# An attention and mixture-of-experts kernel: stage 0's values between its keys, loads in another order, one mask table

## The chip, the cores and the metric

The kernel runs on one core of a Trainium2 chip. The metric is device time in microseconds (us) of one execution. The engines are TensorE (PE for matmuls, PEld for weight loads), VectorE (DVE), ScalarE (ACT), GpSimd (POOL) and SyncE (SP, which only issues DMAs here). GpSimd issues DMAs too, on a queue of its own.

## The reference, cut to what matters

```python
x = x + attention(_gn(x), ...)      # x: (2, 48, 48, 384), float32; _gn: 32 groups over h, w and channels
x = x + experts(_gn(x), ...)

qkv = x @ qkv_w.T + qkv_b           # 12 heads of 32
# 16 register tokens give 16 more keys and values for every query
mask = make_neighbourhood_mask(7, 7, 48, 48)     # 7x7 window, clipped at the borders
scores = einsum('bnqe,bnke->bnqk', q, k_cat) / sqrt(32)
attn = softmax(where(mask_cat, scores, -1e30))
o = einsum('bnqk,bnke->bnqe', attn, v_cat)
return o @ out_w.T + out_b

# experts: 4 experts, hidden size 96 each, softmax router, top 2, gelu
```

## The kernel before, in words

The channels lie on the 128 partitions, 3 blocks of 128 (4 heads) per image. Attention runs in **six stages** (`gi` 0 to 5): stages 0 to 2 are the three head blocks of the first image, 3 to 5 those of the second. A product in fp32 quality is made of three fp16 matmuls per step (high times high, high times low, low times high); so after each projection ScalarE writes the high half from PSUM and VectorE the low half.

The image is cut in six column **tiles** (`s`) of 8 columns, 384 tokens each, and in six row **strips** (`a`) of 8 rows. A stage does this:

- *Keys*, strip by strip (`keys`, TensorE; `keys_high`, ScalarE; `keys_low`, VectorE, which also copies the strip's overlapping windows to `KT`), stored to `kscr` by SyncE. In stage 0 a strip waits for the normalised input (`gn_hi`, `gn_lo_v`), which ScalarE and VectorE are writing strip by strip.
- *Queries*, tile by tile, stored to `qscr` by GpSimd. From stage 1 on the output projection of the stage before (`project_out`) stands between them. In stage 0 ScalarE and VectorE split the other weights there too.
- *Values*, tile by tile, copied out by ScalarE (`values_out`) and stored to `vscr` by GpSimd, three DMAs a tile.
- *Scores against keys, first pass* (`scores`, line 1184): six groups per tile into PSUM, VectorE takes a maximum of each (`maximum`, line 561). After six, `split_maxima` splits them, TensorE turns them (`maxima_turned`), ScalarE copies them (`maxima_out`, tile `MT`) and GpSimd sends them into two rows of `QS` (`maxima_in`), where the second pass subtracts them inside the matmul. Tiles 0 to 2 are done ahead; 3 to 5 inside the loop over strips, in three pairs of steps per tile (`score_units`): tile 4's six in tile 2, tile 5's six in tile 3.
- *Second pass* (`key_scores`, line 1210), exponents on ScalarE (`exps`, line 890), and `weighted` (line 1233), which sums values and, with a matrix of ones, the exponents. VectorE then makes reciprocals and normalises (`reciprocals`, `normalise`).

The order on every engine is the order of the code; nothing is scheduled. SyncE's order in a stage: stores of the keys; then for tiles 0 to 3 keys (`keys_in`) and queries (`queries_in`); queries of tiles 4 and 5; values of tiles 0 and 1 (`values_in`, six DMAs each, waiting for the stores `v_out` of the tile and its right neighbour); then keys of tile 4 (into slot 0, once the second pass of tile 0 is through: `st_mm`), values of 2, keys of tile 5, values of 3, 4, 5. `keys_in` first loads a mask table of 8 rows for tiles 0, 1, 4 and 5, because border tiles have another window. In stage 0 the values of tiles 0 and 1 come before the first scores, and the scores of tile 1 (and 2) wait until the maxima of the tile before are copied (`t_ev`), since they share a bank.

In stages 2 and 5 the input's next normalisation runs beside the tiles: `normalised` (line 493, tile `GT_`) and `low_half` (line 503) on VectorE, two of the three low halves on GpSimd (line 343). GpSimd in stage 0 also adds the output bias to the first image (line 394) and issues the six loads of the second image. After stage 5 comes the experts' layer.

## Time and profile before

| | us |
|---|---|
| three runs | 649.11, 655.11, 649.22 (median 649.22) |
| profiled execution | 652.61, its span 650.8 |
| stage 0: start, keys' matmuls, first values, end | 0, 22.7, 51.4, 106.5 |
| stages 1, 2, 3, 4, 5 begin (rounded) | 106, 182, 265, 340, 417 |
| experts' layer begins (rounded) | 505 |

Granted TensorE clock of the profiled execution: 0.992 of full speed. In the rows further down, a bracket at the end gives the time an engine stood idle before the row and what released it; `SPq` is SyncE's DMA queue of instructions; `ps` is PSUM, `KB` the loaded keys, `QS` the loaded queries with mask and maxima rows, `VR` the loaded values, `MX` the maxima.

### The profile page before, as it was taken

What the parts mean: (1) busy time and instruction counts of PE and PEld (TensorE: products, weight loads), DVE (VectorE), ACT (ScalarE), POOL (GpSimd) and SP (SyncE); (2) the same over time, 40 slices, a digit from 0 to 9 for tenths busy, and PEclk for the clock granted to TensorE, in tenths of its full rate; (3) what the DMA queues carried; (4) which work ended last, traced back from release to release, by engine and by line L of the source; (5) the groups of instructions that cost most, each with busy time, mean ns of one, the idle gap of its engine ahead of it and who ended that gap; (6) DMA issues with size and microseconds to landing.
All of it is one profiled execution on the core that took longest, in us unless ns stands there. A gap on an engine that the chain in (4) does not pass through costs nothing.

```text
span 650.8 us, 22416 instructions
## 1 busy us (share of the span) xinstructions
PE 567.0 (87%) x9227; PEld 396.7 (61%) x9227; DVE 455.8 (70%) x1021; ACT 307.4 (47%) x609; POOL 282.7 (43%) x421
## 2 busy tenths in 40 slices
PE   3578879998899978998899987897987889998998
PEld 2346666677655756657675766655765546665554
DVE  6885575777887689676667767886689886863333
ACT  1762555215633288513563244541578337754221
POOL 3116798254222654436993362223744332413131
PEclk9999999999999999999999999999989999999999
DMA  9869774995339952398527966189551002121213
GB/s 305 188 148 287 201 217 119 230 275 156 98 89 220 256 144 71 87 255 227 154 57 177 260 177 165 35 201 256 170 145 48 2 0 74 38 74 37 74 37 109
DMA packets 131597, 95.44 MB, mean 147 GB/s; under 512 B 67324, under 2 KB 125352, under 8 KB 131496
## 3 DMA queue, kind: packets, MB, share of 16 engines
q1 hardware_dynamic: 121992, 75.18, 44.8%
q0 software_dynamic: 9504, 18.84, 9.3%
q8 instruction: 73, 1.20, 0.8%
q14 instruction: 28, 0.23, 0.1%
HBM read 57.62 MB, written 35.54 MB: 143 GB/s over the span
## 4 chain that ended last, share of the span: by engine, by line
PE 53%; DVE 16%; DMA 9%; SPq 7%; ACT 6%; issue 6%; POOL 2%; ACTq 0%; POOLq 0%; DVEq 0%
PE ps L1070 38%; SPq L271 5%; PE ps L1233 5%; PE ps L1184 4%; DVE MX L561 3%; DMA vscr<-VT 3%; DMA KB<-kscr 3%; PE ps L1210 3%; DVE ST L454 2%; ACT XH L831 2%; ACT PT L890 1%; DVE GT_ L493 1%; DVE SUMT L574 1%; DVE KT L531 1%; DMA kscr<-KT 1%
## 5 line engine op out<-in xcount | busy, mean ns | idle before, releaser
L561 DVE TENSOR_REDUCE MX<-ps 128x2 f32<-128x372 f32 x216 | 108.3, 541 | 63.9 <-PE ps L1184 62.9
L1070 PE MATMUL ps<-XH,WQ 128*128 128x384 f16 x810 | 140.6, 327 | 8.7 <-DVE XH L503 7.8
L1070 PEld LDWEIGHTS ps<-XH,WQ 128*128 128x128 f16 x810 | 77.6, 98 | 62.6 <-ACT XH L831 7.5
L890 ACT ACTIVATE PT<-ps 128x448 f32<-128x448 f32 (+1 forms) x162 | 78.7, 511 | 52.0 <-PE ps L1210 51.6
L1184 PE MATMUL ps<-KB,QS 120*32 120x186 f16 x1728 | 57.8, 250 | 27.0 <-DVE MX L561 10.6
L434 POOL TENSOR_TENSOR KT<-QS,KT 128x384 f16<-128x384 f32 x36 | 34.3, 962 | 95.3 <-ACT KT L983 95.3
L1210 PE MATMUL ps<-QS,KB 122*128 122x112 f16 (+1 forms) x864 | 64.3, 213 | 12.1 <-ACT PT L890 7.7
L1070 PE MATMUL ps<-WQ,XH 128*128 128x128 f16 x972 | 62.4, 222 | 5.2 <-issue 4.9
L381 POOL DMA_DIRECT2D QS<-MT x72 | 37.8, 529 | 59.5 <-ACT MT L880 59.1
L1210 PEld LDWEIGHTS ps<-QS,KB 122*128 122x128 f16 x864 | 43.3, 99 | 33.1 <-ACT PT L890 16.6
L1070 PEld LDWEIGHTS ps<-WQ,XH 128*128 128x128 f16 x972 | 56.0, 99 | 11.2 <-issue 8.8
L1233 PE MATMUL ps<-PT,VR 128*32 128x112 f32 (+1 forms) x1296 | 60.1, 258 | 2.5 <-DMA VR<-vscr 2.5
L1233 PE MATMUL ps<-PT,ONE 128*32 128x112 f32 (+1 forms) x1296 | 59.5, 254 | 0.8 <-issue 0.8
L1070 PE MATMUL ps<-OS,WO 128*128 128x384 f16 x324 | 57.6, 326 | 2.5 <-DVE X L545 1.5
L1070 PE MATMUL ps<-KT,WQ 128*128 128x384 f16 x324 | 58.6, 326 | 0.8 <-DVE X L726 0.5
L1184 PEld LDWEIGHTS ps<-KB,QS 120*32 120x32 f16 x1728 | 31.5, 97 | 43.5 <-DVE MX L561 16.8
L386 POOL TENSOR_TENSOR OS<-ON,OS 128x384 f16<-128x384 f32 x36 | 33.2, 922 | 33.2 <-ACT OS L896 32.9
L719 DVE TENSOR_TENSOR QS<-ps,QS 128x384 f32<-128x384 f32 x36 | 19.7, 555 | 39.1 <-POOL KT L434 14.1
L1070 PEld LDWEIGHTS ps<-OS,WO 128*128 128x128 f16 x324 | 31.0, 98 | 25.0 <-issue 3.0
L1070 PEld LDWEIGHTS ps<-KT,WQ 128*128 128x128 f16 x324 | 30.9, 98 | 23.8 <-DVE X L726 3.4
L394 POOL TENSOR_SCALAR X<-X,SM 128x384 f32<-128x384 f32 x36 | 44.4, 1242 | 0.4
L358 POOL DMA_DIRECT2D qscr<-QT x18 | 13.3, 741 | 71.2 <-DVE QT L537 71.1
(168 smaller groups left out, 1003.3 us busy)
## 6 DMA issues: line engine op xcount, KB each, us to landing
KB<-kscr SPq DMA_DIRECT2D x108, 192.0 KB, 7.0
kscr<-KT SPq DMA_DIRECT2D x72, 192.0 KB, 2.5
VR<-vscr SPq DMA_DIRECT2D x216, 56.0 KB
QS<-qscr SPq DMA_DIRECT2D x108, 96.0 KB, 6.6
out<-X SPq DMA_DIRECT2D x11, 576.0 KB, 3.3
X<-in_x SPq DMA_DIRECT2D x6, 576.0 KB, 7.3
qscr<-QT POOLq DMA_DIRECT2D x18, 192.0 KB, 3.3
qscr<-PT POOLq DMA_DIRECT2D x18, 192.0 KB, 5.3
```

What stands on the lines that cost most here:

```text
L271: sp.dma_start(VR[0:8 * KW, s % 2, a, :], vscr[8 * a:8 * a + 8, CT_ * s:CT_ * s + KW, :]).then_inc(vr_in[s % 2][a // 3], 16)
L381: pool.dma_start(QS[SROWS + part:SROWS + part + 1, :, s * SN:(s + 1) * SN], MT[part * HEADS:(part + 1) * HEADS, s % 2, :]).then_inc(m_in[s ...
L386: nc.gpsimd.tensor_tensor(OS[:, 1, s * SN:(s + 1) * SN], ON[:, s % 2, :], OS[:, 0, s * SN:(s + 1) * SN], ALU.subtract).then_inc(s_["os_lo" ...
L394: nc.gpsimd.tensor_scalar(xs(img, c, s * SN, SN), xs(img, c, s * SN, SN), cols["obx"][:, c:c + 1], None, ALU.add).then_inc(s_["ob_add"], 1)
L434: nc.gpsimd.tensor_tensor(HW[:, m % 2, 1, k, :], HF[:, unit % 2, :], HW[:, m % 2, 0, k, :], ALU.subtract).then_inc(s_["hl"], 1)
L561: V.tensor_reduce(out=MX[:, s % 2, t, 2 * pair:2 * pair + 2], in_=ps[:, S_BANK(s, i), 0:2 * RUN].rearrange("p (h n) -> p h n", h=2), op=AL ...
L719: V.tensor_tensor(HF[:, unit % 2, :], ps[:, 2 + k, 0:SN], GE[:, unit % 2, :], ALU.mult).then_inc(s_["hf"], 1)
L890: A(PTS[n % 4][:, 0:w], ps[:, ST_BANK(n), 0:w], ACT.Exp, scale=SCORE).then_inc(s_["exd"], 1)
L1070: last = mm(bank, lhsT(a, k), rhs(b, k), start=(k == 0 and n == 0), stop=(finish and k == steps - 1 and n == 2))
L1184: last = mm(ps[32 * j:32 * j + 32, S_BANK(s, i), hh * RUN:(hh + 1) * RUN], QS[0:SROWS, h, q0:q0 + 32], KB[0:SROWS, h, slot(s), at:at + RUN ...
L1210: last = mm(ps[:, ST_BANK(n), h * w:(h + 1) * w], KB[0:TROWS, h, slot(s), LEAD + CHUNK * a:LEAD + CHUNK * (a + 1)], QS[0:TROWS, h, s * SN ...
L1233: last = mm(ps[DH * h:DH * (h + 1), bank, CT_ * q0:CT_ * q1], lhsT, PTS[n % 4][:, h * w:(h + 1) * w], start=(a == 0), stop=(a == STRIPS - ...
```

## The change

Five things are changed.

1. In stage 0 the values are made in six blocks of another cut: 16 rows of three tiles instead of one tile (`early_values`). Four blocks follow keys strips 1 to 4, one the first query tile, one the last. Banks are dealt anew for stage 0, and ScalarE's and GpSimd's value copies and stores go between those of the queries.
2. In stage 0 the first scores of tiles 0 to 2 then follow without values between; both first sets of maxima are sent after all value stores.
3. SyncE loads tile 3's keys and queries only after tile 0's scores, then values of tiles 0 and 1, then queries of 4 and 5. The mask tables of `keys_in` are gone: one table stays loaded, and the query side names another row at the borders. The loads of the second image are issued in tiles 3 to 5 of stage 0.
4. In tiles 2 and 3 VectorE takes all six maxima before reciprocals and, in stages 2 and 5, before the normalisation.
5. A key bank is free once VectorE's low half is read (`k_ps`), not after the two window copies (`k_lo`).

TensorE in stage 0, from the first keys strip on, before (`XH,WQ` keys and queries, `WQ,XH` values, `KB,QS` scores of the first pass, `ID,MXH` turned maxima):

```order
L1070 MATMUL ps<-XH,WQ 128x384 x108
L1070 MATMUL ps<-WQ,XH 128x128 x54
L1070 MATMUL ps<-BVH,WO 128x1 x27
L1184 MATMUL ps<-KB,QS 32x186 x48
L1070 MATMUL ps<-WQ,XH 128x128 x54
L1196 MATMUL ps<-ID,MXH 8x128 x3
L1184 MATMUL ps<-KB,QS 32x186 x48
```

and now:

```order
L1080 MATMUL ps<-XH,WQ 128x384 x18
L1080 MATMUL ps<-WQ,XH 128x128 x27
L1080 MATMUL ps<-XH,WQ 128x384 x9
...
L1080 MATMUL ps<-XH,WQ 128x384 x18
L1080 MATMUL ps<-WQ,XH 128x128 x27
L1080 MATMUL ps<-XH,WQ 128x384 x45
L1080 MATMUL ps<-WQ,XH 128x128 x27
L1080 MATMUL ps<-BVH,WO 128x1 x27
L1217 MATMUL ps<-KB,QS 32x186 x72
L1229 MATMUL ps<-ID,MXH 8x128 x3
L1217 MATMUL ps<-KB,QS 32x186 x48
```

The values have moved from between the scores to between keys and queries, and the scores of three tiles stand together.

SyncE's queue in a stage, from the first key load on, before:

```order
L251 DMA KB<-in_ktab 8x4x868
L254 DMA KB<-kscr 32x4x768 x3
L260 DMA QS<-qscr 32x4x384 x3
...
L254 DMA KB<-kscr 32x4x768 x3
L260 DMA QS<-qscr 32x4x384 x9
L271 DMA VR<-vscr 112x1x128 x12
L251 DMA KB<-in_ktab 8x4x868
L254 DMA KB<-kscr 32x4x768 x3
L271 DMA VR<-vscr 112x1x128 x6
```

and now:

```order
L250 DMA KB<-kscr 32x4x768 x3
L256 DMA QS<-qscr 32x4x384 x3
...
L250 DMA KB<-kscr 32x4x768 x3
L256 DMA QS<-qscr 32x4x384 x3
L268 DMA VR<-vscr 112x1x128 x12
L256 DMA QS<-qscr 32x4x384 x6
L250 DMA KB<-kscr 32x4x768 x3
L268 DMA VR<-vscr 112x1x128 x6
```

Six query loads have moved from ahead of the twelve value loads to between them and tile 4's keys; the table load before those keys is gone.

VectorE in stage 2, tile 2, before:

```order
L561 TENSOR_REDUCE MX<-ps 128x2 x3
L493 TENSOR_SCALAR GT_<-X,SM 128x384
L574 STREAM_TRANSPOSE SUMT<-ps 128x384
L575 RECIPROCAL RC<-SUMT 128x12
L561 TENSOR_REDUCE MX<-ps 128x2 x3
L568 TENSOR_SCALAR MXH<-MX 128x3x4
```

and now:

```order
L566 TENSOR_REDUCE MX<-ps 128x2 x6
L573 TENSOR_SCALAR MXH<-MX 128x3x4
L574 SCALAR_TENSOR_TENSOR MXH<-MX,MXH 128x3x4
L497 TENSOR_SCALAR GT_<-X,SM 128x384
L579 STREAM_TRANSPOSE SUMT<-ps 128x384
L580 RECIPROCAL RC<-SUMT 128x12
```

The six maxima stand together, and the normalisation and the reciprocal come behind their split.

The diff, cut:

```diff
+VECTOR, VECTOR_SIX = ((0,), (), (1,), (), (), ()), ((), (), (0,), (1,), (), ())
...
         def kb_count(gi, s):
             if s in (2, 3):
                 return 48 * (gi + 1)
-            return 128 * gi + (64 if s < 2 else 128)
-
-        K_BANK = (4, 6, 2, 3, 5, 7)
-        V_BANK = lambda gi, s: 7 if gi and s == TILES - 1 else 2 + s % 2
-        Q_BANK = lambda s: 2 + s % 2
+            return 96 * gi + (48 if s < 2 else 96)
+        K_BANK = lambda gi, a: (4, 6, 2, 3, 5, 7)[a] if gi else (4, 6)[a % 2]
+        V_BANK = lambda gi, s: (2, 3, 2, 3, 2, 7)[s] if gi else (2, 3, 5, 7, 0, 1)[s]
+        Q_BANK = lambda gi, s: 2 + s % 2 if gi else (4, 6)[s % 2]
...
             def keys_in(gi, s):
-                if s in (0, 1, 4, 5):
-                    kind = {0: 0, 1: 1, 4: 1, 5: 2}[s]
-                    sp.dma_start(KB[112:120, :, slot(s), :], ktab[kind, 16:24].unsqueeze(1).broadcast_to([8, HEADS, SLOTW])
-                                 ).then_inc(kb_in[slot(s)], 16)
...
             def values_in(gi, s):
-                for t in {s, min(s + 1, TILES - 1)}:
+                near = {s, min(s + 1, TILES - 1)}
+                for t in near if gi else [2 * b + half for half in {u // 3 for u in near} for b in range(KC)]:
                     sp.wait_ge(v_out[t], 48 * (gi + 1))
...
-                for s in range(4):
+                for s in range(3):
                     keys_in(gi, s)
                     queries_in(gi, s)
+                sp.wait_ge(s_["s_mm"], 36 * gi + 6)
+                keys_in(gi, 3)
+                queries_in(gi, 3)
+                for s in (0, 1):
+                    values_in(gi, s)
                 for s in (4, 5):
                     queries_in(gi, s)
-                for s in (0, 1):
-                    values_in(gi, s)
...
                 for s in range(TILES):
                     queries_out(gi, s)
-                if gi:
-                    register_values(gi)
-                for s in range(TILES):
+                    if gi == 0 and s > 1:
+                        values_out(0, s - 2)
+                register_values(gi)
+                for s in range(TILES) if gi else (4, 5):
                     values_out(gi, s)
-                    if gi == 0 and s == 1:
-                        register_values(gi)
-                    if s in ((3, 4) if gi == 0 else (2, 4)):
-                        maxima_in(gi, s // 2 - 1 if gi else s - 3)
+                    if gi and s in (2, 4):
+                        maxima_in(gi, s // 2 - 1)
+                if gi == 0:
+                    maxima_in(0, 0)
+                    maxima_in(0, 1)
...
-                        if gi == 0 and a == 3:
-                            c, at = s // 2, s % 2 * 3 * SN
-                            pool.dma_start(xs(1, c, at, 3 * SN), x[1, :, c, at:at + 3 * SN]).then_inc(x_in[1][c][s % 2], 16)
+                        if gi == 0 and s > 2 and a in (1, 4):
+                            c, half = s - 3, a // 4
+                            at = half * 3 * SN
+                            pool.dma_start(xs(1, c, at, 3 * SN), x[1, :, c, at:at + 3 * SN]).then_inc(x_in[1][c][half], 16)
...
             def keys_low(gi, a):
-                link(V.scalar_tensor_tensor(out=KU[:, a % 2, 1, :, 3:3 + W], in0=ps[:, K_BANK[a], 0:SN].rearrange("p (r c) -> p r c", c=W),
+                V.scalar_tensor_tensor(out=KU[:, a % 2, 1, :, 3:3 + W], in0=ps[:, K_BANK(gi, a), 0:SN].rearrange("p (r c) -> p r c", c=W),
...
+                                       op0=ALU.add, op1=ALU.subtract).then_inc(s_["k_ps"], 1)
+                dve.wait_ge(s_["k_ps"], 6 * gi + a + 1)
...
-                        if a == 1 and s:
+                        if a == (3 if s in (2, 3) else 1) and s:
                             reciprocals(gi, s - 1)
...
                         if n:
-                            if a in (0, 2):
-                                normalised(n, s, a // 2)
-                            elif a % 2 and a // 2 not in POOL_K[n]:
-                                low_half(n, s, a // 2)
+                            for k in (VECTOR_SIX if s in (2, 3) else VECTOR)[a]:
+                                normalised(n, s, k)
+                            if a == 5:
+                                low_half(n, s, 1)
...
                 for s in range(TILES):
                     queries_high(gi, s)
+                    if gi == 0 and s:
+                        values_out(0, s - 1)
...
             def queries(gi, s):
                 if s < 2:
-                    pe.wait_ge(s_["k_lo"], 6 * gi + 3 + s)
+                    pe.wait_ge(s_["k_ps"], 6 * gi + (3 if gi else 5) + s)
...
                 for j in range(KC):
-                    if 0 < s < TILES - 1:
+                    if s == 0:
+                        pe.wait_ge(s_["k_ps"], 6 * gi + (8, 11, 12)[j])
+                    elif s < TILES - 1:
...
+            def early_values(e):
+                if e == 4:
+                    pe.wait_ge(s_["kr_lo"], 1)
+                if e == 5:
+                    pe.wait_ge(s_["vr_sb"], 1)
+                b, first = e // 2, 3 * (e % 2)
+                for i in range(KC):
+                    at = (first + i) * SN + b * P
+                    last = split_product(ps[:, V_BANK(0, e), P * i:P * (i + 1)], lambda a, k: xh1(a, k, at, P),
+                                         lambda q, k: WQ[:, 0, q, k, 2 * P:3 * P])
+                last.then_inc(s_["v_mm"], 1)
...
                 if i == 0 and s in (1, 2):
-                    pe.wait_ge(s_["t_ev"], 6 * gi + (s if gi == 0 else s - 1))
+                    if 6 * gi + s - 1 > 0:
+                        pe.wait_ge(s_["t_ev"], 6 * gi + s - 1)
...
+                if gi == 0 and s == 0:
+                    if i == 0:
+                        pe.wait_ge(s_["q_lo"], 6)
+                    if 0 < i < 5:
+                        pe.wait_ge(s_["v_sb"], i + 2)
...
+                    if gi == 0 and 0 < a < STRIPS - 1:
+                        early_values(a - 1)
                 for s in range(TILES):
                     queries(gi, s)
...
+                    if gi == 0 and s == 0:
+                        early_values(4)
...
                 if gi == 0:
-                    all_values(0)
-                    all_values(1)
-                    value_bias()
-                    all_scores(0)
-                    all_values(2)
-                    all_values(3)
-                    maxima_turned(0, 0)
...
+                    early_values(5)
                     value_bias()
...
+                for k in range(6):
+                    for i in range(3):
+                        scores(gi, k // 2, 3 * (k % 2) + i)
+                    if k in ((3, 5) if gi else (2, 4)):
+                        maxima_turned(gi, k // 2 - 1)
+                    if gi:
+                        for b in range(KC):
+                            values(gi, k, b)
...
-        out[16 + c, :, :, c] = BIG
+        out[16 + max(c, 3), 0, :, c] = BIG
+        out[16 + c, 1:TILES - 1, :, c] = BIG
+        out[16 + min(c, 4), TILES - 1, :, c] = BIG
```

## Rows read from the trace of the kernel before

**Rows 1.** Page, parts 1, 2 and 6: busy time, DMA share in 40 slices, query loads.
```profile
PE 567.0 (87%) x9227; PEld 396.7 (61%) x9227; DVE 455.8 (70%) x1021; ACT 307.4 (47%) x609; POOL 282.7 (43%) x421
...
DMA  9869774995339952398527966189551002121213
...
QS<-qscr SPq DMA_DIRECT2D x108, 96.0 KB, 6.6
```

**Rows 2.** Instructions in time (start, us, engine, line; waited, releaser): TensorE, stage 0.
```profile
36.10 1.62 PE L1070 MATMUL ps<-XH,WQ 128*128 128x384 f16 x9 [1.71 <-DVE XH L503]
...
69.16 1.68 PE L1070 MATMUL ps<-WQ,XH 128*128 128x128 f16 x27
...
74.29 0.36 PE L1233 MATMUL ps<-PT,VR 128*32 128x88 f32 x8
...
83.03 0.50 PE L1184 MATMUL ps<-KB,QS 120*32 120x186 f16 x16 [1.33 <-DMA KB<-kscr]
```

**Rows 3.** Busy by stretch: PE, PEld, DVE, ACT, POOL; clock, DMA share, GB/s.
```profile
51.40:71.40 20.00, 15.79 (x339) 14.09 (x339) 10.21 (x26) 3.93 (x10) 12.46 (x23) 0.91 1.02 286
...
62.00:63.00 1.00, 0.59 (x17) 0.62 (x21) 0.04 (x1) 0.15 (x1) 0.91 (x2) 0.50 1.11 255
```

**Rows 4.** Waits of TensorE: total us, times, longest.
```profile
PE ps L1184 <- DVE MX L561: 10.6, 12, 1.8
...
PE ps L1184 <- DMA KB<-kscr: 6.7, 6, 1.7
...
PE ps L1070 <- DVE KT L531: 1.0, 2, 0.7
```

**Rows 5.** Instructions in time: VectorE, stage 0.
```profile
55.53 2.81 DVE L561 TENSOR_REDUCE MX<-ps 128x2 f32<-128x372 f32 x6
```

**Rows 6.** Instructions in time: GpSimd, stage 0.
```profile
52.62 0.71 POOL L358 DMA_DIRECT2D qscr<-QT  x1 [0.38 <-DVE QT L537]
...
58.71 1.57 POOL L365 DMA_DIRECT2D vscr<-WR  x3 [0.64 <-ACT WR L874]
...
63.66 1.04 POOL L381 DMA_DIRECT2D QS<-MT  x2
```

**Rows 7.** Instructions in time: SyncE's queue, stage 0.
```profile
63.89 9.49 SPq L271 DMA_DIRECT2D VR<-vscr  x12
...
76.02 2.12 SPq L254 DMA_DIRECT2D KB<-kscr  x3
```

**Rows 8.** Instructions in time: SyncE's queue, stage 1.
```profile
135.43 5.92 SPq L260 DMA_DIRECT2D QS<-qscr  x9
...
145.91 8.43 SPq L271 DMA_DIRECT2D VR<-vscr  x12
...
154.38 0.48 SPq L251 DMA_DIRECT2D KB<-in_ktab  x1
...
154.91 1.44 SPq L254 DMA_DIRECT2D KB<-kscr  x3
```

**Rows 9.** Chain that ended last, stage 1 (start, us, what).
```profile
140.17 5.68 DMA vscr<-VT
```

**Rows 10.** DMA issues from 150 to 170 us: times, KB, us to landing.
```profile
vscr<-VT POOLq DMA_DIRECT2D x3, 64.0 KB, 2.2
```

**Rows 11.** Instructions in time: TensorE, stages 1 and 5.
```profile
163.03 0.34 PE L1184 MATMUL ps<-KB,QS 120*32 120x186 f16 x8 [0.44 <-DVE MX L561]
...
166.96 0.50 PE L1184 MATMUL ps<-KB,QS 120*32 120x186 f16 x16 [1.23 <-DMA KB<-kscr]
...
454.71 0.81 PE L1184 MATMUL ps<-KB,QS 120*32 120x186 f16 x15 [3.43 <-issue]
```

**Rows 12.** Instructions in time: TensorE, stage 2.
```profile
243.37 0.34 PE L1184 MATMUL ps<-KB,QS 120*32 120x186 f16 x8 [1.77 <-DVE MX L561]
```

**Rows 13.** Instructions in time: VectorE, stage 2.
```profile
234.53 0.47 DVE L493 TENSOR_SCALAR GT_<-X,SM 128x384 f32<-128x384 f32 x1
...
240.51 1.47 DVE L493 TENSOR_SCALAR GT_<-X,SM 128x384 f32<-128x384 f32 x1
```

84 lines of the change are left out of this document (34 added, 50 removed).

## The prediction

> **What bounds the kernel now.** I read the page first, then the busy time by stretch, the instructions of each engine in order of time, the waits, and the chain that ended last. TensorE is busy 87% of the span [rows 1], so a microsecond can be gained only where TensorE stands still or where its work moves under something else. The reader should look for two things: how long TensorE stands before a row, and which engine or queue releases it.
>
> In stage 0 the keys are made in six strips. TensorE multiplies 1.62 us and then stands 1.71 us for VectorE's normalised strip [rows 2]. There are five such gaps, four of them of 1.71 us. From the end of the queries (51.4) to the first score against keys (71.4) TensorE holds the values of six tiles and the scores of three. The scores of tiles 1 and 2 each wait for the maxima of the tile before to be turned and copied. But look at the DMA column of that stretch: it is at 1.02 of the engines' time and 286 GB/s [rows 3]. This stretch is full for the DMA engines too, and that is what most of my doubt hangs on.
>
> In the stages after, TensorE's waits are of three kinds: score maxima on VectorE (10.6 us in 12 waits), the loads of key tiles 4 and 5 (6.7 us in 6) [rows 4], and stalls whose releaser the profile does not show, the longest 3.43 us [rows 11]. The last kind comes and goes between executions and I give the change nothing for it. The tail of the program (from 505 us, the second layer) is not touched.
>
> **Part 1: values of stage 0 between the keys.** Six blocks of 27 matmuls, 1.68 us each [rows 2], leave the stretch after 51.4. Four go into the 1.71 us gaps, where they just fit (1.62 + 1.63 to 1.68 against a period of 3.33): free, if nothing slows the strips. The last two still cost their 1.6 us each, one among the queries and one behind them. With weights, queries and value copies on ScalarE and VectorE in one line, the queries should end about 2.8 us later than now, near 54; that is 1.6 for the block and the rest for queries that now wait for a low half behind a weight split. TensorE then needs only the six score groups of each tile, and the pace is VectorE's: 2.81 us of maxima [rows 5] and 0.4 of splitting, 3.2 per tile. Three tiles from 56 end at 66, against 71.4 now. So the naive gain is 5 us, or 8 with the queries unshifted.
>
> I take 3.0, since two queues come last instead. GpSimd issues every store of values in three pieces, 1.57 us per group [rows 6], and now has six of these and six query stores of about 0.7 each behind one another before the first two maxima: 14 to 15 us of issuing from about 47 to 50, so the maxima go out at about 63.5. Before, the first went out at 63.66 [rows 6]: no earlier. Second, the loads of values for tile 0 used to wait for two stores and began at 63.89 [rows 7]; because a block now holds 16 rows of three tiles, they need blocks 0, 2 and 4, the last of which leaves GpSimd near 62 and lands 2.2 us later on quiet engines [rows 10], or 5.7 on full ones [rows 9]. So they begin between 64 and 67.6. The first weighted sum, at 74.29 now [rows 2], can come at about 71.5. Tile 4's keys, which TensorE waited for at 83.03 [rows 2], were issued at 76.02 [rows 7]; the value loads and now two query tiles stand ahead of them, and the six loads of the second image no longer collide with them. They come 1 to 2 us earlier. Ends for this part: 0 (the stores land at 67.6 and everything follows as today) and -8. The value nearest to the rows of the two queues is -3.0.
>
> **Part 2: load order and one mask table, all six stages.** A table load costs the queue 0.53 us before tile 4's keys (154.38 to 154.91) and the same before tile 5's [rows 8]. Against that, the six loads of query tiles 4 and 5 now stand between the values of tile 1 and the keys of tile 4. Nine such loads took 5.92 us, so six are up to 3.9, or 2.9 at the pace of the three key loads that took 1.44 [rows 8]. Net: tile 4's keys 2.4 to 3.4 later, if the value loads begin when they do now. They should not: they began at 145.91, right when the store of tile 1's values landed, 5.68 us after its issue [rows 8, 9], and such a store lands in 2.2 us when the engines are not full [rows 10]. With six query loads of 96 KB [rows 1] out of the way, at 286 KB per us [rows 3], the engines clear 2.0 us sooner, and some 0.5 more for the two tables ahead of tiles 0 and 1. Both effects nearly cancel at tile 4; tile 5's table load and the shorter backlog leave about 0.4 per stage over five stages. I take -2.0. Ends: -5.3, all key waits after stage 0 (6.7 less 1.33) [rows 2, 4], and +17 (3.4 in each of five).
>
> **Part 3: maxima of tiles 4 and 5 back to back.** In tiles 2 and 3 the reciprocals stand between two batches of three maxima. TensorE waits 0.44 for that [rows 11], in four stages, twice each: 3.5 us. In the first tile of each pair the next key load is what ends last (1.23 us at 166.96) [rows 11], so that gain is eaten there. I take half, -1.8; ends 0 and -3.5.
>
> **Part 4: the second image's normalisation in stages 2 and 5.** There the same wait is 1.77 us [rows 12], and there are four like it, two per stage: 10.6 less 3.5 leaves 7.1 us for them. Between the maxima stands not only the reciprocal but a normalisation that took 1.47 us, while the same instruction six microseconds earlier took 0.47 [rows 13]. The order rows show that it moves behind all six maxima. TensorE's waits should go, but tile 5's keys land close behind and VectorE has hardly a pause in these tiles, so I take -4.0; ends 0 (the keys come last) and -7.1. The Trainium skill (SBUF — State Buffer, "SBUF: two separate sides") says VectorE and GpSimd lock a shared port pair against each other, the loser blocking for the whole instruction. The trace agrees in the 1.47 against 0.47 beside a running GpSimd subtraction; by that rule the moved instruction also becomes 1 us shorter, and the sum would take the whole 7.1.
>
> **Part 5: earlier release of key banks.** The low half now frees its bank before the two window copies. TensorE waited for those copies 1.0 us in two places [rows 4]. I take -0.5, ends 0 and -1.0. The added wait on VectorE for its own result replaces one of the same kind: 0.
>
> **Hidden or moved at nothing.** The six loads of the second image go later but are read only in stage 1; the bias additions cover them. The new semaphore waits on TensorE behind value copies come on banks whose copies were finished one query earlier.
>
> Sum: -3.0 - 2.0 - 1.8 - 4.0 - 0.5 = -11.3 us. The profiled execution took 652.6, the median of the runs is 649.2; the profiled one holds a 3.43 us unexplained stall [rows 11], which accounts for the difference. On the median: 649.2 - 11.3 = 637.9, so **638 us**; a profile like the one before would take 641. Taking the doubts of parts 1 and 4 on either side, this case's own range is 633 to 644.
>
> **The rivals.**
>
> *Tile 4's keys come late (slower).* The value stores land no earlier, and the two query tiles ahead push the keys back by 2.8 (between 2.4 and 3.4) in each of five stages: +14, of which stages 2 and 5, where nothing waits for this tile now, absorb about 1 each: +12. The parts that rely on tile 5's keys halve: -0.9 and -2.0; stage 0 and the bank keep -3.5. Total +5.6: 655 to 656 us. It decides from the point where the store lands less than 2.4 us earlier than today. For it: value loads begin with a landing and are then a solid 8 us of issuing. Against it: the store lands just as the DMA's full stretch ends: of the 40 slices of 16.3 us, the one up to 146 has a 9 and the one behind it a 5 [rows 1]. Chance 0.10. The Trainium skill (DMA: Bandwidth & Descriptors, "Queues, rings and completion order") says each DMA engine takes packets in turn from the queues that have work. By that rule a store on GpSimd's queue does not stand behind the SyncE backlog, so taking loads off that backlog would help less, which is this rival. The 5.68 us against 2.2 shows a share, not a bypass.
>
> *Stage 0 opens up.* The maxima pace holds and stores land fast since fewer loads compete: part 1 is -8 and part 2 is -3.5: 649.2 - 8 - 3.5 - 1.8 - 4.0 - 0.5 = 631.4. Chance 0.14.
>
> *Most of it is hidden (about no change).* The DMA stretch at full share stays what ends stage 0, tile 5's keys swallow parts 3 and 4, and TensorE's clock falls in the new sparse stretch, where it has 1.1 us of work in every 3.2. After 1.7 us of standing still it was granted 0.50, the 1.2 GHz level, at 62 [rows 3]; a first tile at that level would add up to 3 us. Then -3 to -4 is left: 646. Chance 0.18.
>
> The forecast keeps 0.58. **Range:** leaving out the slow rival and the far end of the fast one, 630 to 652. About 1% (6.5 us) is what a measurement here tells from no change: faster means under 642.7, slower over 655.7. Faster: 0.50 of the forecast, 0.13 of the fast rival: 0.63. Slower: most of the first rival and a little of the rest: 0.09. Same: 0.28.
>
> **What will show it.** Part 1: key strips still 3.33 us apart with values between, and the first weighted sum at 71 to 72. Part 2: in stage 1 the value loads begin at a time 2 to 2.5 us earlier relative to the end of the queries, and the wait for tile 4's keys stays near 1 us. If it is over 2.5, the slow rival holds. Parts 3 and 4: no wait for maxima over 0.5 us left, and the normalisation at 0.47 us. I am wrong if TensorE stands as long as before in stage 0 or if the waits for maxima turn into waits for keys.

## The result and the profile after: slower

The changed kernel took 662.6 us (median of 4 runs, 661.2 to 666.8) beside 650.4 us for the kernel before on the same chip: a ratio of 1.0171, with a 95% interval of 1.013 to 1.0212. The forecast was 638 us and its range ended at 652, so both were wrong. Nearest to what came is the slow rival (655 to 656 us): tile 4's keys come late. Its size was too small, and its premise, that the value stores land no earlier, held only in part. Timed again later, the same kernel gave 1.0148 (1.0098 to 1.0198). Ratios in this document leave out executions that fell into a slower state (six of eleven for k1 below, one of five for h2), while the times in us are medians of all.

The profiled execution took 662.64 us, with a span of 660.8 us at a mean granted clock of 0.941 (before: 650.8 at 0.992). The first lines of its page, to be laid beside [rows 1]:

```profile
PE 581.1 (88%) x9227; PEld 411.7 (62%) x9227; DVE 447.9 (68%) x1021; ACT 308.2 (47%) x609; POOL 284.4 (43%) x421
...
PEclk8798679999799998899899998999987899999999
DMA  9769347995319853098534965349662001120212
```

TensorE has the same number of instructions and is busy 14.1 us longer, so they ran at a lower clock. In the DMA row the fifth and sixth slices (65 to 98 us), both 7 in [rows 1], are 3 and 4. Part of that is only work that moved: four of the six loads of the second image were issued there before (76.97 to 93.79), and now the first goes out at 96.30. The waits of TensorE say what it stands for. Columns: total us, times, longest.

```profile
PE ps L1217 <- DMA KB<-kscr: 20.0, 6, 4.5
PE ps L1243 <- ACT PT L895: 10.7, 17, 2.0
...
PE ps L1243 <- DMA QS<-MT: 5.6, 3, 2.8
...
PE ps L1217 <- DVE MX L566: 4.5, 10, 1.5
```

Against [rows 4] the waits for score maxima fell from 10.6 to 4.5 us, which is what parts 3 and 4 were after (but b1 below, which lacks both, has 5.5 us of them). The waits for loaded keys rose from 6.7 to 20.0 us. All six stand before tile 4's first scores, one per stage. SyncE's queue and TensorE in stage 1 (start, us; in brackets the wait and its releaser):

```profile
140.98 2.22 SPq L250 DMA_DIRECT2D KB<-kscr  x3
143.24 1.40 SPq L256 DMA_DIRECT2D QS<-qscr  x3
149.58 8.42 SPq L268 DMA_DIRECT2D VR<-vscr  x12
158.04 3.14 SPq L256 DMA_DIRECT2D QS<-qscr  x6
161.23 1.39 SPq L250 DMA_DIRECT2D KB<-kscr  x3
```

```profile
161.80 0.53 PE L1243 MATMUL ps<-QS,KB 122*128 122x88 f16 x8
166.84 0.81 PE L1217 MATMUL ps<-KB,QS 120*32 120x186 f16 x16 [4.52 <-DMA KB<-kscr]
167.44 0.59 PE L1266 MATMUL ps<-PT,VR 128*32 128x112 f32 x8
```

The fourth row of the queue is the six query loads, 3.14 us of issuing right ahead of tile 4's keys. The chain of waits runs through just these: the store of tile 1's values, twelve value loads, six query loads, the keys' landing.

```profile
144.40 5.12 DMA vscr<-VT
149.58 0.71 SPq L268
...
162.18 4.62 DMA KB<-kscr
166.80 0.04 issue
166.84 0.81 PE ps L1217 x11
```

To compare stages of kernels I count from the first matmul of a stage's own keys (in stage 1 at 107.40 before and 111.63 after). The table has the start of the value loads and of tile 4's keys on SyncE's queue so counted, in us. "Again" is a second profile of the changed kernel, a2 the version of the next section that only puts the six query loads back.

| | stage 1 | 2 | 3 | 4 | 5 | mean |
|---|---|---|---|---|---|---|
| value loads, before | 38.51 | 41.13 | 38.85 | 40.31 | 42.04 | 40.17 |
| changed | 37.95 | 39.38 | 36.64 | 38.26 | 39.95 | 38.44 |
| changed, again | 36.43 | 40.26 | 37.46 | 38.00 | 41.24 | 38.68 |
| a2 | 37.76 | 39.19 | 37.03 | 39.05 | 40.32 | 38.67 |
| keys of tile 4, before | 47.51 | 50.13 | 48.25 | 49.29 | 53.12 | 49.66 |
| changed | 49.60 | 51.90 | 48.92 | 50.95 | 51.75 | 50.62 |
| changed, again | 49.11 | 52.08 | 50.28 | 51.16 | 52.57 | 51.04 |
| a2 | 46.22 | 47.65 | 45.78 | 47.52 | 48.78 | 47.19 |

The value loads do begin sooner than before, by 1.7 us in the mean (0.6 to 2.2) and 1.5 in the second profile (0.8 to 2.3), where the forecast had 2.0 to 2.5. But they begin just as soon in a2. Tile 4's keys are issued 1.0 and 1.4 us later than before, and 3.4 and 3.9 later than in a2. (In stage 5 of the kernel before they are late by another cause: they wait 1.9 us for TensorE's work on tile 0, behind the stall of 3.43 us.) TensorE takes the keys up 2.9, 1.3, -0.1, 1.7 and 1.9 us later than before in stages 1 to 5. In stage 3 it used to come to tile 4 only 0.38 us before the keys were there; now it is there 4.12 us before them. What it gains ahead of tile 4 is waited away at that place.

The stretches around that store and behind the wait, in the columns of [rows 3]:

```profile
144.40:149.50 5.10, 5.10 (x124) 4.52 (x125) 3.23 (x8) 1.59 (x4) 4.46 (x10) 1.00 0.68 200
...
166.80:172.80 6.00, 5.96 (x124) 5.08 (x125) 3.42 (x9) 0.98 (x2) 0.00 (x0) 0.50 0.60 149
```

and the stretch in which the same store was under way before, 5.68 us long [rows 9]:

```profile
140.20:145.90 5.70, 4.76 (x109) 4.06 (x107) 3.33 (x8) 1.45 (x3) 4.19 (x8) 1.00 1.10 302
```

Two things are to be seen. First, with the six query loads gone from ahead of it, the DMA share while the store of stage 1 is under way fell from 1.10 to 0.68, and the store took 5.12 us instead of 5.68. That one is the slowest of this profile, though. The same store where it lies on the chain that ended last in other stages (start, us to landing), before in stages 3 and 4:

```profile
298.13 5.80 DMA vscr<-VT
374.36 5.53 DMA vscr<-VT
```

in the changed kernel in stage 4:

```profile
385.27 3.92 DMA vscr<-VT
```

and in its second profile in stages 1, 4 and 5:

```profile
145.37 3.60 DMA vscr<-VT
386.79 3.65 DMA vscr<-VT
467.75 5.64 DMA vscr<-VT
```

So the store mostly lands sooner, by up to 2.2 us, and not always. Second, in the 6 us behind the wait of 4.52 us the granted clock was 0.50, the 1.2 GHz level: the group of eight at 167.44 takes 0.59 us, and the same group at full clock before, at 160.03, took 0.36.

Stage 0, TensorE:

```profile
68.59 0.82 PE L1243 MATMUL ps<-QS,KB 122*128 122x88 f16 x8 [2.50 <-DMA QS<-MT]
...
72.45 0.52 PE L1266 MATMUL ps<-PT,VR 128*32 128x88 f32 x8 [1.00 <-ACT QT L895]
...
84.92 0.81 PE L1217 MATMUL ps<-KB,QS 120*32 120x186 f16 x16 [2.91 <-DMA KB<-kscr]
...
105.81 0.52 PE L1243 MATMUL ps<-QS,KB 122*128 122x88 f16 x8 [2.79 <-DMA QS<-MT]
```

The first weighted sum comes 1.84 us sooner than in [rows 2], but tile 4's keys come 1.89 us later, and near the end of the stage TensorE waits 2.79 us for maxima. GpSimd issues those. Bias additions and loads of the second image stood around the last maxima before too; now two of these loads, of 576 KB each, go out in the 3.7 us right ahead of them, and the chain has 5.19 us from the maxima's issue to their landing:

```profile
96.30 0.64 POOL L430 DMA_DIRECT2D X<-in_x  x1
96.97 2.46 POOL L395 TENSOR_SCALAR X<-X,SM 128x384 f32<-128x384 f32 x2
99.39 0.58 POOL L430 DMA_DIRECT2D X<-in_x  x1
99.97 1.04 POOL L382 DMA_DIRECT2D QS<-MT  x2
```

Stage lengths in us, before and after: stage 0 106.5 and 110.7; 1: 75.3 and 78.9; 2: 83.3 and 85.3; 3: 74.5 and 76.0; 4: 76.9 and 78.8; 5: 88.8 (with the 3.43 us stall of [rows 11]) and 85.7; the rest the same. Stages 0 to 4 are all longer; stage 5, which held the stall before, is shorter.

### The profile page after: what moved, and what is told of

The parts are those of the page before. It is cut to its first block, busy times and chain, and to the rows that moved or that the text cites. A ratio compares the mean times of both kernels' runs of the same rounds, so it can differ in the third digit from the quotient of the medians.

```text
span 660.8 us, 22403 instructions
## 1 busy us (share of the span) xinstructions
PE 581.1 (88%) x9227; PEld 411.7 (62%) x9227; DVE 447.9 (68%) x1021; ACT 308.2 (47%) x609; POOL 284.4 (43%) x421
## 4 chain that ended last, share of the span: by engine, by line
PE 63%; DVE 10%; DMA 9%; ACT 5%; SPq 5%; issue 4%; POOL 3%; ACTq 0%; POOLq 0%; DVEq 0%
PE ps L1080 42%; PE ps L1266 8%; PE ps L1217 5%; PE ps L1243 4%; DMA KB<-kscr 3%; SPq L268 3%; DVE ST L458 2%; ACT PT L895 2%; POOL vscr L366 2%; DMA QS<-MT 1%; DMA vscr<-VT 1%; DVE MX L566 1%; ACT XH L836 1%; DMA X<-in_x 1%; SPq L250 1%
## 5 line engine op out<-in xcount | busy, mean ns | idle before, releaser
L1080 PE MATMUL ps<-XH,WQ 128*128 128x384 f16 x810 | 143.0, 331 | 3.1 <-DVE PT L542 1.3
L895 ACT ACTIVATE PT<-ps 128x448 f32<-128x448 f32 (+1 forms) x162 | 78.6, 510 | 76.4 <-PE ps L1243 76.2
L1217 PE MATMUL ps<-KB,QS 120*32 120x186 f16 x1728 | 62.2, 266 | 28.3 <-DMA KB<-kscr 20.0
L1243 PE MATMUL ps<-QS,KB 122*128 122x112 f16 (+1 forms) x864 | 68.5, 224 | 18.8 <-ACT PT L895 10.7
L1243 PEld LDWEIGHTS ps<-QS,KB 122*128 122x128 f16 x864 | 47.2, 105 | 41.1 <-ACT PT L895 18.9
L1266 PE MATMUL ps<-PT,VR 128*32 128x112 f32 (+1 forms) x1296 | 64.8, 277 | 3.1 <-DMA VR<-vscr 1.6
L1266 PE MATMUL ps<-PT,ONE 128*32 128x112 f32 (+1 forms) x1296 | 63.5, 272 | 0.0
L1217 PEld LDWEIGHTS ps<-KB,QS 120*32 120x32 f16 x1728 | 34.0, 101 | 43.4 <-DMA KB<-kscr 20.9
L1080 PE MATMUL ps<-WQ,XH 128*128 128x128 f16 x972 | 60.5, 220 | 0.0
```

The lines of the kernel that those rows point to most:

```text
L895: A(PTS[n % 4][:, 0:w], ps[:, ST_BANK(n), 0:w], ACT.Exp, scale=SCORE).then_inc(s_["exd"], 1)
L1080: last = mm(bank, lhsT(a, k), rhs(b, k), start=(k == 0 and n == 0), stop=(finish and k == steps - 1 and n == 2))
L1217: last = mm(ps[32 * j:32 * j + 32, S_BANK(s, i), hh * RUN:(hh + 1) * RUN], QS[0:SROWS, h, q0:q0 + 32], KB[0:SROWS, h, slot(s), at:at + RUN ...
L1243: last = mm(ps[:, ST_BANK(n), h * w:(h + 1) * w], KB[0:TROWS, h, slot(s), LEAD + CHUNK * a:LEAD + CHUNK * (a + 1)], QS[0:TROWS, h, s * SN ...
L1266: last = mm(ps[DH * h:DH * (h + 1), bank, CT_ * q0:CT_ * q1], lhsT, PTS[n % 4][:, h * w:(h + 1) * w], start=(a == 0), stop=(a == STRIPS - ...
```

## The experiments

All ratios are to the kernel before, run beside each version on the same chip (647.9 to 658.6 us in these runs). "T" is tile, "Q" the query loads of tiles 4 and 5.

| version | us | ratio | 95% interval |
|---|---|---|---|
| changed kernel | 662.6 | 1.0171 | 1.0130 to 1.0212 |
| the same, again | 662.2 | 1.0148 | 1.0098 to 1.0198 |
| a1 old order of loads | 645.7 | 0.9892 | 0.9858 to 0.9927 |
| a2 only Q back ahead of the values | 640.8 | 0.9820 | 0.9761 to 0.9879 |
| a3 only T3 at once again | 660.6 | 1.0122 | 1.0070 to 1.0174 |
| b1 kernel before + new order of loads | 665.3 | 1.0185 | 1.0142 to 1.0229 |
| c1 changed + filler; again | 659.6; 659.7 | 1.0100; 1.0101 | 1.0066 to 1.0134; 1.0059 to 1.0143 |
| c2 a2 with maxima as before | 644.3 | 0.9873 | 0.9808 to 0.9938 |
| c3 a2 without early values | 643.4 | 0.9853 | 0.9786 to 0.9921 |
| d1 a2 + stores reordered | 639.1 | 0.9802 | 0.9734 to 0.9871 |
| g1 d1 + filler | 643.4 | 0.9866 | 0.9820 to 0.9913 |
| h1 kernel before + one table | 648.3 | 0.9916 | 0.9881 to 0.9950 |
| h2 h1 + T3 deferred | 641.6 | 0.9836 | 0.9773 to 0.9899 |
| h3 h1 + maxima and bank release | 645.7 | 0.9868 | 0.9816 to 0.9921 |
| k1 d1 + T5's queries behind T4's keys | 650.5 | 0.9861 | 0.9806 to 0.9916 |

### Which part of the new order costs the time: a1, a2, a3, b1

**Theory:** the six query loads between the values and tile 4's keys. **Rivals:** the new arrangement of stage 0, and the deferral of tile 3's loads. In a2 the edit is:

```diff
                 keys_in(gi, 3)
                 queries_in(gi, 3)
-                for s in (0, 1):
-                    values_in(gi, s)
                 for s in (4, 5):
                     queries_in(gi, s)
+                for s in (0, 1):
+                    values_in(gi, s)
```

a1 also loads tile 3 at once, as before; a3 does only that. b1 puts the new order (with T3 deferred and Q behind the values) into the kernel before and changes nothing else.

a1: 

> The changed kernel with SyncE's load order put back (tile 3 and the queries of 4 and 5 right behind tile 2, values after them); all else of the change stays. Theory T (the six query loads between the values and tile 4's keys make those keys late, and the clock falls in the wait): tile 4's keys wait falls from 20.0 us in six waits to under 7, and the time is 643 to 648. Rival R (stage 0's new arrangement and its queues are what costs): stays over 656. Rival C (deferring tile 3 is the cost, the queries do not matter): also 643 to 648; the next two kernels tell it from T.

a2: 

> The changed kernel with only the queries of tiles 4 and 5 moved back ahead of the values; tile 3 stays deferred until tile 0's scores. T: SyncE issues them in its pause before the stores of values land, tile 4's keys come about 3 us earlier per stage, time 645 to 650. Rival C: tile 3's load still meets the stores, so values begin late, time 657 to 663.

a3: 

> The changed kernel with only tile 3 loaded at once; the queries of 4 and 5 stay behind the values. T: the store of tile 1's values lands earlier by 1 to 2 us (less traffic than before), but the six loads keep their 3.2 us ahead of tile 4's keys: 652 to 659. Rival C: 643 to 648.

b1: 

> The kernel before with only the load order of the change (tables still loaded). T: slower than before by 10 us or more, 658 to 668, with long waits for tile 4's keys. Rival R: within 2 us of before.

The pattern leaves no doubt: every version with Q behind the values is at 1.01 or over, every one with Q ahead is under 0.992, whatever the rest. Alone in the old kernel (b1) the new order gives 1.0185, as much as the whole change. Two expectations were missed in size: a2 came out 4 us below the lowest time named for it, a3 some 2 us above the highest. SyncE's queue in a2, stage 1, and TensorE's wait there:

```profile
137.04 5.26 SPq L256 DMA_DIRECT2D QS<-qscr  x9
144.16 8.41 SPq L268 DMA_DIRECT2D VR<-vscr  x12
152.62 2.46 SPq L250 DMA_DIRECT2D KB<-kscr  x3
```

```profile
158.12 0.50 PE L1217 MATMUL ps<-KB,QS 120*32 120x186 f16 x16 [0.89 <-DMA KB<-kscr]
```

Counted from the stage's first keys (106.40) the value loads begin at 37.76, in the changed kernel at 37.95, and in the mean of five stages at 38.67 against 38.44 and 38.68: with the six loads ahead of them they are no later. The keys are issued at 46.22 and not at 49.60. Where tile 3 is loaded at once, the moved queries do buy something in front: the value loads begin at 39.61 in a1 and at 38.48 in a3 (means), but the keys go out at 48.29 and at 50.96. So beside the deferral of tile 3 moving the queries bought nothing at the front and cost 3.4 to 3.9 us at the back. By the ratios that is 21 to 23 us from a2 to the changed kernel (0.9820 to 1.0148 and 1.0171), and 15 us from a1 to a3; the forecast's far end for part 2 was +17. In the profiles each of stages 0 to 4 is 2.6 to 5.2 us longer than in a2 (105.5, 74.9, 80.6, 72.7 and 76.2 us there). The rival of stage 0's arrangement falls with b1, that of the deferral with a3 and a2: with Q ahead, deferring tile 3 does not cost, as a1, without it, is 4.7 us slower than a2. (With Q behind, a3 is 1.7 to 3.2 us faster than the changed kernel, within the intervals.)

b1 has the tables still and none of the other parts, and yet it is as slow as the changed kernel, though with Q ahead the maxima (3.1 and 3.5 us) and the table (5.5 us) alone are worth some 9 us (below). One reason shows in its waits for maxima, which are short without any reordering (10.6 us in the kernel before):

```profile
PE ps L1187 <- DVE MX L564: 5.5, 8, 1.8
```

With TensorE at a lower clock behind each wait for keys, VectorE keeps up, and reordered maxima have less to gain. That is a reading of the two profiles; no run was made for it.

### Does the clock matter: c1, g1, and both again

**Theory clock:** what TensorE loses at 0.50 behind each wait adds to the loss. Rival: behind the wait other engines set the pace anyway. The edit keeps TensorE multiplying until the keys are there; the filler's result is overwritten.

```diff
                 if i == 0 and s == 4:
+                    pe.wait_ge(s_["mx"], 36 * gi + 23)
+                    for _ in range(20):
+                        mm(ps[:, S_BANK(4, 0), 0:SN], WO[:, 0, 0, 0:P], WO[:, 0, 0, :], start=True, stop=True)
```

c1: 

> The changed kernel with 20 extra matmuls (384 columns each, results not used, some 3.2 us) on TensorE just ahead of its wait for tile 4's keys in each stage. They add work only to time in which it stands. Clock theory (part of the loss is the clock that falls to the 1.2 GHz level in these waits of 2 to 4.5 us, then a slow tile of some 2 us more): granted clock of tile 2 stays near 1.00 and the time falls by 5 to 12 us, to 650 to 657. Rival (the waits alone make the loss; the keys come when they come): the same time within 2 us, 660 to 665, or slower.

The changed kernel, again: 

> The changed kernel unaltered, timed again beside the version with filler matmuls on one chip. It should stand at 1.012 to 1.022 of the kernel before (660 to 665 us), with 18 to 22 us of waits for tile 4's keys in six places. It is the base for the next kernel: clock theory, 3 to 6 us above it; theory without clock, within 1.5 us of it.

(It has 25.4 us of waits for keys in seven places, more than expected.)

c1, again: 

> The changed kernel with 20 filler matmuls (their result is overwritten) ahead of each wait for tile 4's keys. Theory clock (part of the loss is matmuls at the 1.2 GHz level after TensorE has stood for the keys): 3 to 6 us less than the unaltered changed kernel of this call. Rival no clock (the filler only fills a wait, and what comes behind it is bound by VectorE): within 1.5 us of it.

g1: 

> The changed kernel with query tiles 4 and 5 ahead of the values and the stores of stage 0 in the order 0, 2, 4, 1, maxima, 3, maxima, 5, and with filler matmuls in the pauses of stage 0's scores, before its first weighted sums' key scores and ahead of tile 4's scores in each stage. Theory clock: 2 to 4 us less than the same kernel without filler (639), so 635 to 637, ratio 0.973 to 0.978. Rival no clock: 638 to 641, since these waits are already short (about 1 us for each key tile).

In c1's second profile the filler stands in the wait, and the clock behind it holds (columns of [rows 3]):

```profile
160.49 3.42 PE L1189 MATMUL ps<-WO 128*128 128x384 f16 x20
164.84 0.50 PE L1221 MATMUL ps<-KB,QS 120*32 120x186 f16 x16 [0.94 <-DMA KB<-kscr]
165.17 0.37 PE L1270 MATMUL ps<-PT,VR 128*32 128x112 f32 x8
```

```profile
164.80:170.80 6.00, 5.48 (x171) 4.29 (x171) 4.85 (x12) 2.35 (x5) 0.00 (x0) 1.00 0.63 155
```

By the ratios the filler took off 3.1 us beside the changed kernel timed with it and 4.6 us against its first timing; the intervals overlap both times. The mean is 3.8 us, not settled apart from zero. It misses the first expectation (5 to 12) and lies at the low end of the second (3 to 6). The page shows why it is not more. In that profile the 9,227 other matmuls are busy 587.2 less the filler's 20.5, so 566.7 us, 11.5 less than in the unfilled run beside it (578.2):

```profile
PE 587.2 (89%) x9347; PEld 410.1 (62%) x9347; DVE 448.1 (68%) x1021; ACT 307.7 (47%) x609; POOL 285.2 (43%) x421
```

Of 11.5 us saved in TensorE's busy time 3.9 came off the span (663.5 to 659.6); the rest went into other waits (maxima at the first scores 5.4 us instead of 3.7, the loads of queries 4.8 instead of 2.5, stalls without a releaser 6.1 instead of 2.4). g1 is d1 with eight filler matmuls ahead of tile 4's scores in each stage and 32 more in stage 0. There the key waits were already 1.5 us or less, and it gave 0.9866 against 0.9802 for d1; the intervals overlap, so it is no faster and perhaps slower. The miss against the clock theory's 635 to 637 is plain, and the 643.4 us lie above the rival's range too. That a pause shorter than the filler is lengthened by it would fit, but so would g1's stalls without a releaser, 7.7 us beside d1's 2.9; no run tells them apart.

### What the other parts are worth: c2, c3, h1, h2, h3

c2 puts the reciprocals and the second image's normalisation back between the maxima, c3 takes the early values out, both with Q ahead. h1 is the kernel before with one thing changed:

```diff
             def keys_in(gi, s):
-                if s in (0, 1, 4, 5):
-                    kind = {0: 0, 1: 1, 4: 1, 5: 2}[s]
-                    sp.dma_start(KB[112:120, :, slot(s), :], ktab[kind, 16:24]...)
```

h2 adds the deferral to it, h3 the reordered maxima and the earlier bank release.

```diff
-                for s in range(4):
+                for s in range(3):
                     keys_in(gi, s)
                     queries_in(gi, s)
+                sp.wait_ge(s_["s_mm"], 36 * gi + 6)
+                keys_in(gi, 3)
+                queries_in(gi, 3)
```

c2: 

> The kernel with the queries ahead of the values (a2_queries_first, 640.8), and in it reciprocals and the normalisation of the second image put back between the maxima, as before the change. If the waits for maxima were worth what the rows say (7.1 us in stages 2 and 5, 3.5 in the others, as far as keys do not eat it): 644 to 651. If they are hidden by the key loads: within 2 us of 641.

c3: 

> The kernel before with all of the change but the early values of stage 0 and what hangs on them (copies, stores, two sets of maxima, loads of the second image), and with the queries of 4 and 5 ahead of the values. It gives the early values' worth against a2_queries_first. If they gain the 1 to 2 us that stage 0's length shows: 641 to 644. If they gained 5 us or more: 646 or over. If they cost: under 640.

h1: 

> The kernel before with only the one mask table: the four small table loads per stage are gone, the order of all other loads is the old one. Part 2's reckoning (0.53 us less ahead of tile 4's keys and ahead of tile 5's, in five stages, where the keys end last): 1 to 3 us less than before, ratio 0.995 to 0.998. Rival hidden: within 0.7 us of it. If the rest of the gain of the good order comes from the tables alone: 5 us or more.

h2: 

> The kernel before with the one mask table and with tile 3's keys and queries loaded only once tile 0's scores are done; query tiles 4 and 5 stay ahead of the values, everything else is old. Theory D (the deferral by itself is worth some 5 us): 4 to 6 us below the version with the table alone (0.9916), ratio 0.983 to 0.986. Rival E (the deferral gains only where early values or reordered maxima are present): 0.990 to 0.993.

h3: 

> The kernel before with the table, the reordered maxima and the early bank release, with the old order of all loads and no early values. Theory D: the maxima are worth 3 to 4 us in either order of loads, so 3 to 4 us below the table alone: ratio 0.985 to 0.987. Rival E (maxima and deferral gain only together): within 1 us of the table alone, 0.990 to 0.993.

The table alone is worth 5.5 us (interval 3.3 to 7.8), more than the 1 to 3 that part 2's reckoning gave; it is the last of the three cases named for h1. Table and deferral together give 10.7 us (6.6 to 14.9), so two small edits of the order hold nearly all that a2 gains. The maxima are worth 3.1 us in the old order (h1 to h3) and 3.5 us in the good one (c2 to a2), where 5.8 were reckoned. Early values give 2.2 us in the good order (c3 to a2) and lose 1.6 in the old one (h3 to a1). Single intervals are 3 to 5 us to either side, so only the table, and table with deferral, are settled by themselves; for the maxima two pairs agree; for early values the sign is open.

What the deferral, and perhaps the table, gain from may be a class of waits that I had set aside: those for which the profile names no releaser ("issue"). The waits of TensorE in h2 (columns as above) still hold the maxima and the keys; the two rows of stalls are 1.4 and 0.8 us.

```profile
PE ps L1183 <- DVE MX L560: 10.3, 12, 1.8
...
PE ps L1183 <- DMA KB<-kscr: 5.3, 8, 1.6
...
PE ps L1069 <- issue: 1.4, 1, 1.4
...
PE ps L1183 <- issue: 0.8, 1, 0.8
```

In the kernel before these stalls are 12.6 us in all. Summed over TensorE's lines for each profile without filler:

| | stalls without a releaser, us |
|---|---|
| kernel before (tables, T3 at once) | 12.6 |
| T3 at once, no tables: h1, h3, a1, a3 | 6.4, 11.2, 7.6, 5.8 |
| T3 deferred, tables kept: b1 | 4.8 |
| T3 deferred, no tables: h2, c2, c3, a2, d1, k1, changed, again | 2.2, 0.6, 2.5, 1.7, 2.9, 3.2, 0.6, 2.4 |

The two groups without tables do not overlap, and the means, 7.8 and 2.0, differ by 5.8 us, about the 4.7 and 5.2 that the deferral is worth (a1 to a2, h1 to h2). Three things speak for caution. The profiles with filler, with tile 3 deferred and no tables, have 5.2, 6.1 and 7.7 us of such stalls. h1 and h3 have the same loads and 6.4 and 11.2 us, so what the table does to the stalls is not shown. And there is a rival that was not tried: in both pairs the deferral also lets tile 4's keys be issued 1.1 us sooner in the mean of five stages (48.29 to 47.19, 48.37 to 47.27), and the table alone 1.3 us sooner (49.66 to 48.37), which over five stages is of the same size as the gains.

Four of the longest stalls before lie in the full stretch of the DMA engines (share 1.02 to 1.08). The one of 3.43 us, in the columns of [rows 3]:

```profile
451.30:454.70 3.40, 0.00 (x0) 0.00 (x0) 0.51 (x1) 0.17 (x1) 1.57 (x3) 0.96 1.08 251
```

The engines' queues carry instructions too. In the eight us around that stall the view of the queues shows:

```profile
q1 hardware_dynamic: 1686, 1.59, 88.3%
q0 software_dynamic: 198, 0.45, 19.2%
q8 instruction: 1, 0.02, 1.0%
```

A possible reading is that TensorE's instruction loads queue behind the kernel's own transfers, and that tile 3's six loads and the tables filled the stretch in which they come. The groups show that, filler apart, the stalls go with the loads; that it is the instruction transfer that is late was not tried by itself. The one instruction packet near the stall says little, since the page counts 73 of them over the span, before and after alike. Three smaller stalls, of 0.81, 0.66 and 0.65 us, lie where the share is 0.3 to 0.4, so a full stretch is not the cause of all.

### Queue or landing: d1 and k1

d1 issues stage 0's stores in the order in which the value loads wait for them. k1 takes one query tile out from ahead of the value loads and puts it behind tile 4's keys:

```diff
-                for s in (4, 5):
-                    queries_in(gi, s)
+                queries_in(gi, 4)
                 for s in (0, 1):
                     values_in(gi, s)
...
                     values_in(gi, s + 2)
+                    if s == 0:
+                        queries_in(gi, 5)
```

d1: 

> a2_queries_first with GpSimd's order in stage 0 changed: value blocks 0, 2 and 4, which the first value loads wait for, are stored first, then 1, maxima of tile 0, block 3, maxima of tile 1, block 5. If GpSimd's queue is what ends last in stage 0, the wait for the first maxima (3.7 us) halves and stage 0 is 1.5 to 3 us shorter: 638 to 639.5. If the DMA engines are, no change: 640 to 642.

k1: 

> The best version so far (queries 4 and 5 ahead of the values, reordered stores in stage 0), with query tile 5's three loads of queries behind tile 4's keys and tile 2's values. If SyncE's queue sets when the value loads begin: they begin 1.5 to 2 us earlier and 1 to 5 us are gained. If the landing of tile 1's values sets it (in that version the queue stands before the value loads with nothing issued): no change, within 2 us of it, ratio 0.978 to 0.983.

d1 has the lowest ratio of all, 0.9802, but is only 1.2 us under a2 and within its interval; its stage 0 is 0.8 us shorter, not 1.5 to 3, and the wait for the first maxima falls from 3.7 to 2.5 us. k1's value loads begin at 36.75 from the stage's first keys in stage 1, d1's at 37.97, but in the mean of five stages at 38.88 and 38.83: no sooner, so it is not SyncE's queue that they wait for. No time was gained: 0.9861 against 0.9802, some 4 us more, with overlapping intervals, and both expectations for the time missed. The moved loads stand ahead of some keys wherever they go, and this time it is tile 5's (TensorE, stage 1 of k1):

```profile
156.04 0.50 PE L1223 MATMUL ps<-KB,QS 120*32 120x186 f16 x16 [0.64 <-DMA KB<-kscr]
...
163.90 0.81 PE L1223 MATMUL ps<-KB,QS 120*32 120x186 f16 x16 [2.09 <-DMA KB<-kscr]
```

Its waits for keys are 18.3 us in all, d1's 6.9, though k1's profile is of one of its longer executions (span 649.7). It looks like the same fault a second time, with three loads and one tile later; with overlapping intervals that is not shown.

## Why the prediction was wrong

**Part 2 failed, in one step:** the sentence "With six query loads of 96 KB [rows 1] out of the way, at 286 KB per us [rows 3], the engines clear 2.0 us sooner", so that both effects "nearly cancel at tile 4". The step gives 2.0 us in front to the moving of the queries. The runs put nothing in its place: the value loads begin at 38.67 in a2 and at 38.44 and 38.68 in the changed kernel (means of five stages). They do begin 1.5 to 1.7 us sooner than before, but that comes with the deferral and the table and is there without moving the queries. The gains in front were counted as if they added up; with tile 3 deferred the six loads no longer held up the store. The price on the other side was about right: I had 2.4 to 3.4 us per stage, and from the start of the value loads to the keys it is 2.7 to 3.7 us more than before in stages 1 to 4. So the two did not cancel: tile 4's keys are issued 1.0 to 1.4 us later than before, and 3.4 to 3.9 later than they would be in a2.

That the store takes 5.68 us because the DMA engines are full, and 2.2 when they are quiet [rows 9, 10], was read from two rows that differ in more than that. With less traffic it took 3.6 to 3.9 us three times and 5.1 and 5.6 twice. What decides between these was not found.

The rival said it "decides from the point where the store lands less than 2.4 us earlier". So it did, with 1.5 to 1.7, though its own premise was that the stores land no earlier. The Trainium skill (DMA: Bandwidth & Descriptors, "Queues, rings and completion order") has each DMA engine serve the queues with work in turn. The trace agrees with that rule as far as it goes: GpSimd's store landed somewhat sooner when SyncE's backlog shrank, but by less than I had reckoned from the bytes taken away. No run tests the rule by itself. I should have given the rival far more than 0.10: the cancellation rested on one untried landing time, while the six issues ahead of the keys were certain.

**The rival's size** was 7 us short (its own sum gives 654.8). It had 2.8 us per stage over five stages less 2, and halves for parts 3 and 4. Stages 1 to 4 are 3.6, 2.0, 1.5 and 1.9 us longer, a little less than it had; but it left stage 0 out, which is 4.2 us longer, with a wait of 2.91 us for tile 4's keys, and it kept 6.4 us of gains from the other parts. Of these next to nothing is seen: b1, which has none of them and the tables besides, is as slow as the changed kernel. What comes ahead of tile 4's scores is waited away there (stage 3 above); for the maxima, which come behind, the cause is only argued. The clock, which I had named only for stage 0, may add some 3.8 us; two pairs of timings agree on the sign and neither is settled.

**Part 1** was nearly right in its places: first weighted sum at 72.45 (71 to 72 forecast), GpSimd's maxima at 63.5, strips 3.32 to 3.33 us apart after the first two. Its claim that tile 4's keys come 1 to 2 us earlier in stage 0 failed with part 2 (84.92 after 83.03); in a2 TensorE takes them up at 81.95. Its -3.0 stands beside -2.2 and +1.6, unsettled.

**Parts 3 and 4** were mis-sized: -5.8 against 3.1 and 3.5 measured (h1 to h3 also holds part 5). With Q ahead the waits for maxima at the first scores fall by 5.5 us in both pairs (10.1 to 4.6 and 9.7 to 4.2), so some two us of that do not reach the time. The normalisation that took 1.47 us in tile 2 [rows 13] takes 0.47 behind the six maxima:

```profile
253.43 0.47 DVE L497 TENSOR_SCALAR GT_<-X,SM 128x384 f32<-128x384 f32 x1
```

But a wait of 1.45 us in stages 2 and 5 stayed, though I had said none over 0.5:

```profile
257.42 0.35 PE L1217 MATMUL ps<-KB,QS 120*32 120x186 f16 x8 [1.45 <-DVE MX L566]
```

**Part 5** (-0.5) was not run alone; TensorE's wait for the window copies [rows 4] is gone from the list.

**The table** was priced only by what it stands ahead of, and is worth 5.5 us by itself. The sentence that failed there is that of the stalls, "I give the change nothing for it": they do not just come and go: filler apart, they were fewer in every profile with tile 3 deferred. Had the six loads stayed where they were, the change would have been a2: 0.982 of 649.2 is 637.5, beside a forecast of 638. That agreement is partly luck: table and deferral hold 10.7 of it, of which the forecast had a few us at most.

## What to carry to other kernels

When loads are moved in a queue that issues in order, first count what now stands ahead of the load that is waited for at the moment of that wait; this is certain. A gain from "the engines clear sooner" needs a row that shows the awaited transfer faster at a lower share, not just one fast and one slow transfer, and two changes that both clear the same stretch must not be added up. Look at every stage: stage 1 alone would have said that the loads begin no sooner, and that k1's begin 1.2 us sooner; the mean of five says otherwise both times. And small loads can matter: taking out four tables a stage, of 0.3 to 0.5 us of issuing each, gave 5.5 us, more than any other single part of the change is shown to give.

## What the runs showed of the hardware

The store of tile 1's values, in pieces of 64 KB, landed in 5.53 to 5.80 us beside the nine query loads of the old order, and in 3.60, 3.65, 3.92, 5.12 and 5.64 us with six of them gone. At a DMA share of 0.68 it still took 5.12, so the share alone does not set it. After waits of 2.0 to 4.5 us TensorE was granted 0.50 in the following 6 us in stages 0 and 1 and 0.61 to 0.72 in the others (second profile: 0.52 to 0.61 after 3.4 to 5.4 us, 1.00 after 2.12 us); 20 filler matmuls, 3.42 us in all, in the wait kept it at 1.00 in stage 1. Yet 11.5 us less busy time of TensorE brought only 3.9 us of span in one pair of profiles. And stalls of TensorE that no semaphore explains were 12.6 us before and 0.6 to 3.2 in the eight profiles without filler in which tile 3's loads were deferred and the tables gone.
